# The second chunk's gate and up sums and masked product made in the opening stage, in two down banks, with first-pass weights in four slots

## The reference

```python
scores = softmax(x @ gate_w.T)                       # 64 experts in 8 groups of 8
w_e    = scores of the 8 largest, 0 elsewhere
flat   = w_e[:, inv_map];  scalar = flat.sum(-1)      # one number for each token and group
soft   = softmax(where(flat == 0, -1e9, flat), axis=-1)
xg = x[:, None, :] + einsum('ngi,ghi->ngh', soft, mask_up_w)
g  = einsum('ngh,gih->ngi', xg, gate_proj_w)          # 352 columns for each of 8 groups
u  = einsum('ngh,gih->ngi', xg, up_proj_w)
d  = einsum('ngi,ghi->ngh', silu(g) * u, down_proj_w)
y  = einsum('ng,ngh->nh', scalar, d)
```

## Time and profile before

| | us |
|---|---|
| median of 3 runs | 1887.09 |
| the profiled execution's own time | 1890.33 |
| its span, first to last instruction | 1888.6 |
| PE busy | 1857.5 |
| DVE busy | 801.9 |
| ACT busy | 527.9 |
| POOL busy | 128.2 |

### The profile page before, as it was taken

One profiled execution on the slowest core, in us unless ns is written; L12 is line 12 of the kernel. 1 busy time (PEld: TensorE's weight loads), 2 busy tenths in 40 slices (PEclk: granted clock), 3 DMA queues, 4 the chain that ended last, 5 costly groups with the idle time before them and its releaser, 6 DMA issues.

```text
span 1888.6 us, 22836 instructions
## 1 busy us (share of the span) xinstructions
PE 1857.5 (98%) x8896; PEld 1551.5 (82%) x8896; DVE 801.9 (42%) x1478; ACT 527.9 (28%) x801; POOL 128.2 (7%) x224
## 2 busy tenths in 40 slices
PE   5999999999999999999999999999999999999998
PEld 4888888888888888888888888888888888888887
DVE  5555554545354544323334455354544324322222
ACT  3334422533124432112212533123432111311111
POOL 1121110000000100000010000000000000000000
PEclk9999999999999999999999999999999999999999
DMA  5877786445664456576576555564455566567664
GB/s 169 309 266 262 277 292 207 153 149 176 209 222 157 151 168 205 182 257 210 209 246 220 168 191 167 187 231 167 157 171 178 203 237 212 207 227 254 224 235 160
DMA packets 93131, 390.68 MB, mean 207 GB/s; under 512 B 11584, under 2 KB 11968, under 8 KB 70496
## 3 DMA queue, kind: packets, MB, share of 16 engines
q1 hardware_dynamic: 54096, 286.74, 43.1%
q10 hardware_dynamic: 27600, 47.15, 9.1%
q0 software_dynamic: 11328, 55.32, 7.4%
HBM read 347.36 MB, written 41.81 MB: 206 GB/s over the span
## 4 chain that ended last, share of the span: by engine, by line
PE 95%; DVE 3%; ACT 1%; issue 1%; DMA 1%; SPq 0%; POOL 0%; DVEq 0%; ACTq 0%
PE bank L975 27%; PE bank L977 27%; PE bank L976 27%; PE bank L1203 4%; PE bank L985 1%; PE bank L1146 1%; PE bank L1145 1%; PE bank L1138 1%; PE bank L1132 1%; PE bank L1190 0%; DVE act_t L620 0%; PE bank L1191 0%; PE bank L1005 0%; PE bank L1022 0%; PE bank L1006 0%
## 5 line engine op out<-in xcount | busy, mean ns | idle before, releaser
L975 PE MATMUL bank<-x_hi,wt 128*128 128x512 f32 x1408 | 557.1, 396 | 2.7 <-ACT sig L554 2.7
L977 PE MATMUL bank<-x_lo,wt 128*128 128x512 f32 x1408 | 549.7, 390 | 0.0
L976 PE MATMUL bank<-x_hi,wt 128*128 128x512 f32 x1408 | 549.3, 390 | 0.0
L620 DVE TENSOR_TENSOR act_t<-bank,sig 128x512 f32<-128x512 f32 x176 | 121.6, 691 | 565.7 <-PE bank L1203 556.0
L977 PEld LDWEIGHTS bank<-x_lo,wt 128*128 128x128 f32 x1408 | 264.6, 188 | 56.9
L975 PEld LDWEIGHTS bank<-x_hi,wt 128*128 128x128 f32 x1408 | 265.0, 188 | 55.0 <-issue 2.9
L976 PEld LDWEIGHTS bank<-x_hi,wt 128*128 128x128 f32 x1408 | 265.1, 188 | 52.3
L975 PE MATMUL bank<-dt,a_hi 128*128 128x512 f32 x704 | 279.2, 397 | 0.3 <-DVE a_lo L620 0.3
L977 PE MATMUL bank<-dt,a_hi 128*128 128x512 f32 x704 | 275.1, 391 | 0.0
L976 PE MATMUL bank<-dt,a_lo 128*128 128x512 f32 x704 | 274.2, 389 | 0.0
L554 ACT ACTIVATE sig<-bank 128x512 f32<-128x512 f32 x176 | 105.4, 599 | 484.2 <-PE bank L1203 484.1
(11 more groups left out here) (168 smaller groups left out, 1709.6 us busy)
## 6 DMA issues: line engine op xcount, KB each, us to landing
wt<-scr_w SPq DMA_DIRECT2D x154, 1152.0 KB, 5.2
dt<-scr_d SPq DMA_DIRECT2D x154, 512.0 KB, 5.1
s_bc<-scr_s ACTq DMA_DIRECT2D x128, 256.0 KB, 5.3
scr_w<-wt POOLq DMA_DIRECT2D x22, 1152.0 KB, 6.5
state<-wat POOLq DMA_DIRECT2D x28, 512.0 KB, 5.4
b_all<-wgu SPq DMA_DIRECT2D x22, 512.0 KB, 5.5
scr_d<-dt POOLq DMA_DIRECT2D x22, 512.0 KB, 5.4
s_bc<-scr_s ACTq DMA_DIRECT2D x32, 192.0 KB, 4.7
```

The source lines that it names most:

```text
L620: return nc.vector.tensor_tensor(dst, a, b, op)
L975: mm(dst, wh, xh, start=start, stop=False)
L976: mm(dst, wl, xh, start=False, stop=False)
L977: return mm(dst, wh, xl, start=False, stop=stop)
```

## The change

Five edits, all in phase 0 but the third:

- `masked(1)` and both sums of chunk 1 move from the loop into the opening stage. The sums go to `YB[0]` and `YB[1]` (`g_bank`, `u_bank`), which are free until the first `down`; `down(0)` therefore moves behind both sums of chunk 2 and runs just ahead of `down(1)`.
- High and low gate/up weights of the first pass lie in four slots (`first_w`: two of `wt`, two of `tw`) where they had two; the mask parts stay in two. Chunk 2's weights are split in the opening stage (`gu_hi(2)`, `gu_lo(2)`). The store is now two DMAs, `store_w` (1 MB) and `store_m` (128 KB).
- Router step 46 makes the transposes, the copy and the store of the group sums, ahead of the group softmax rows (49, 50); step 51 is gone, and the sum itself (`scal`) moves from the end of step 46 to the end of step 44 on DVE. This holds for all phases.
- A one-column Silu (`warm`) right behind the Exp of the opening stage.
- The load of block 1 (1 MB, `x_t[1]`) moves from the opening stage to behind `raw(2)` on SP's queue; that of block 2 stays behind `raw(4)`.

```diff
+        def g_bank(n):
+            return YB[0] if n == 1 else GB
+        def u_bank(n):
+            return YB[1] if n == 1 else UB
+        def first_w(c):
+            return (wt, tw)[c % 4 // 2][:, c % 2, 0:2 * GW]
...
@@ SP @@
             raw(1)
-            sp.dma_start(xr(1), x_t[1]).then_inc(ld_x[1], 16)
             for c in range(2, CH):
                 raw(c)
+                if c == 2:
+                    sp.dma_start(xr(1), x_t[1]).then_inc(ld_x[1], 16)
                 if c == 4:
                     sp.dma_start(xr(2), x_t[2]).then_inc(ld_x[2], 16)
@@ POOL @@
             for c in range(CH):
-                store(c)
+                if c == 0:
+                    store_w(0)
+                if c + 1 < CH:
+                    store_w(c + 1)
+                store_m(c)
                 store_d(c)
@@ ACT @@
-            for k in range(43, SLOTS):
-                router(0, k)
+            router(0, 43)
+            gu_hi(2)
+            router(0, 45)
+            act.wait_ge(pool_init, 1)
+            nc.scalar.activation(warm[:], mhalf[:, 0:1], ACT.Silu)
+            router(0, 46)
+            m_top(1)
             load_s(0)
+            router(0, 49)
+            router(0, 50)
             load_s(1)
...
-                    if p == 0 and 0 < c < CH - 1:
+                    if p == 0 and 1 < c < CH - 1:
                         gu_hi(c + 1)
...
-                    if p == 0 and c + 1 < CH:
+                    if p == 0 and 0 < c < CH - 1:
                         m_top(c + 1)
@@ DVE @@
             m_mask(0)
-            router(0, 43)
-            router(0, 44)
             m_rest(0)
-            for k in range(45, SLOTS):
+            m_mask(1)
+            for k in range(43, SLOTS):
                 router(0, k)
+            m_rest(1)
+            gu_lo(2)
...
-                    if p == 0 and c + 1 < CH:
+                    if p == 0 and 0 < c < CH - 1:
                         m_mask(c + 1)
                         m_rest(c + 1)
@@ PE @@
+            router(0, 43)
+            masked(1)
             pe.wait_ge(perm_ok, 4)
-            for k in range(43, SLOTS):
-                router(0, k)
+            router(0, 44)
+            main(g_bank(1), 0, 0, 1)
+            router(0, 46)
+            main(u_bank(1), P, 0, 1)
+            router(0, 49)
+            router(0, 50)
...
-                    if n:
-                        pe.wait_ge(sig_ok, n)
+                    if n > 1:
+                        pe.wait_ge(sig_ok, n if n > 2 else 1)
                         main(GB, 0, p, c)
-                    soft(GB, 0, p, c).then_inc(g_ok, 1)
+                    soft(g_bank(n), 0, p, c).then_inc(g_ok, 1)
...
+                    if n == 2:
+                        pe.wait_ge(sig_ok, 2)
+                        pe.wait_ge(t1_ok, 2)
+                        down(0)
+                    if n > 1:
                         down(n - 1)
                     pieces(3 * n + 2)
-                    if p == 0 and c + 1 < CH:
+                    if p == 0 and 0 < c < CH - 1:
                         masked(c + 1)
```

More of the change, by code:

```diff
@@ L124, in build @@
         ms = sb("ms", [P, NT])
+        warm = sb("warm", [P, 1])
         rr = sb("rr", [P, NT])
@@ L161, in build @@
         d_in = [sem(f"d_in{i}") for i in range(2)]
-        st_w = [sem(f"st_w{i}") for i in range(2)]
+        st_w = [sem(f"st_w{i}") for i in range(4)]
+        st_m = [sem(f"st_m{i}") for i in range(2)]
         st_d = [sem(f"st_d{i}") for i in range(2)]
@@ L239, in load_w @@
                 n, half = p * CH + c, c % 2
+                if p == 1 and c < 4:
+                    sp.wait_ge(st_w[c], 16 * len(range(c, CH, 4)))
                 if p == 1 and c < 2:
-                    sp.wait_ge(st_w[half], 16 * HALF)
+                    sp.wait_ge(st_m[half], 16 * HALF)
                 sp.wait_ge(u_ok, n - 1)
@@ L290, in rstd_of, with store_w, store_m @@
                 pool.wait_ge(rstd_ok, (r + 1) * NT)
-            def store(c):
-                half = c % 2
+            def store_w(c):
                 pool.wait_ge(gu_lo_ok, c + 1)
+                pool.dma_start(scr_w[c][:, 0:W_M], first_w(c).bitcast(F32)).then_inc(st_w[c % 4], 16)
+            def store_m(c):
                 pool.wait_ge(m_ok, c + 1)
-                pool.dma_start(scr_w[c], wt[:, half, :].bitcast(F32)).then_inc(st_w[half], 16)
+                pool.dma_start(scr_w[c][:, W_M:WW], wt[:, c % 2, W_M:WW].bitcast(F32)).then_inc(st_m[c % 2], 16)
             def store_d(c):
@@ L397, in t_hi @@
                     act.wait_ge(v_mm, 2 * t + 2)
+                elif t == 0:
+                    act.wait_ge(u_ok, CH)
+                    act.wait_ge(st_w[2 + s], 16 * len(range(2 + s, CH, 4)))
                 elif s == S_V:
-                    wait(act, k_mm, t * H)
-                elif t:
+                    act.wait_ge(k_mm, t * H)
+                else:
                     act.wait_ge(wo_ok, t * NT)
@@ L553, in silu @@
                 wait(act, t1_ok, n)
-                nc.scalar.activation(sig[:], GB[:], ACT.Silu).then_inc(sig_ok, 1)
+                nc.scalar.activation(sig[:], g_bank(n)[:], ACT.Silu).then_inc(sig_ok, 1)
             def round_a(n):
@@ L1023, in router @@
                     ins.then_inc(flat_ok, 1)
-                elif k in (49, 50, 51):
+                elif k == 46:
+                    pe.wait_ge(scal_ok, p + 1)
+                    for j in range(NT):
+                        ins = nc.tensor.transpose(W1[0:G, cols(j)], scal[:, j, :], ident[:])
+                    ins.then_inc(scalT_ok, 1)
+                elif k in (49, 50):
                     i = k - 49
@@ L1194, in main @@
             def main(b, c0, p, c):
-                hi, lo, _ = weights(c)
+                hi, lo = weights(p, c)
                 for k in range(KC):
```

78 lines of the change are left out of this document (38 added, 40 removed).

## The result

The changed kernel takes 1883.97 us (median of 22 runs, 1881.85 to 1888.72) against 1887.14 (22 runs, 1886.38 to 1893.75). The medians differ by 3.2 us. The ratio is 0.9981, 0.19% less, with a 95% interval of 0.9975 to 0.9986, that is 2.6 to 4.7 us.

The account below looks back on a forecast made before the run. PE was taken to bound the kernel, busy 1857.5 of 1888.6 us. The walk's 6.2 us gain, cut to 5.65 at chunk 3 and 4.95 at chunk 5, gave 1887.09 - 4.9 = 1882.2, range 1880.0 to 1884.9.

Parts of the forecast that it names:

- The end of routing: Opening stage: step 44 at 27.1 us, PE filled with moved work, all four `soft` products done at 36.6.
- The group row: Group sums copied near 32.9 us, multiply of chunk 0 at 38.4, 3.9 earlier; no drain of 1.38 counted.
- The wait that takes their place: Ahead of chunk 2's `soft`: PE idle from 40.35 to 47.1 us for `m_rest(2)`, 6.7 against 11.7 before.
- The clock: Behind chunk 2's idle spell: low for 3.1 us as before; restored at once 1.6 shorter, low twice as long 1.6 longer.
- Chunk 3's load behind the block: Gate/up load on SP's queue: issued at 42.0 us, landing 12.7 later; `soft` of chunk 3 at 61.7, gain 5.65.
- From ACT's start to PE's `soft`: At chunk 3, from the landing of its weights to PE's `soft`: 7.0 us, from 6.95 in the earlier trace.
- The same again at chunk 5: Load behind the second block: issued at 61.3 us, landing at 74.7, `soft` at 81.7, gain down to 4.95.
- Edits at nothing: Split store, moved `scal`, step 46's copy in later phases: no cost; last two, uncovered, under 0.5 us at one chunk.
- Rival 1: Weights of chunks 3 and 5 late, landings of 12.7 to 13.4 us; gain 4.3 to 5.6, 1881.5 to 1882.8; chance 0.50.
- rival 3: Gain mostly given back by longer loads, low clock or late group row; gain 1 to 3.7 us; chance 0.16.
- Rivals 2, 4 and 5: No collision at the block, 1879.3 to 1880.9 (0.24); nothing gained (0.05); slower through chunk 3's load stalling ACT (0.05).

Follow-up runs that it names:

- m_first: The changed kernel with `m_rest(2)` made between the two multiplications of chunk 0, not behind chunk 1's splits; 1885.25 us, ratio 0.9985.
- The fill: x_open plus 24 products of no use on PE in the idle spell ahead of chunk 2's `soft`; 1880.38 us, ratio 0.9958.
- m_store_ahead: The changed kernel with each chunk's mask store queued ahead of the next chunk's 1 MB store; 1883.29 us, ratio 0.9975.
- after_again: The changed kernel timed again with no edit; 1883.95 us, ratio 0.9982.
- after_third: The changed kernel timed a third time with no edit; 1884.14 us, ratio 0.9983.
- x_open: The changed kernel with block 1's load back in the opening stage; 1883.34 us, ratio 0.998.
- m_first_x_open: The changed kernel with the edits of m_first and x_open together; 1876.63 us, ratio 0.9944.
- m_first_gu3: m_first with chunk 3's gate/up load issued ahead of `raw_d(2)` and the block, once `gu_lo(1)` is done; 1877.39 us, ratio 0.9938.
- sums_only: The kernel before plus only the earlier group sums (`scal` in step 44, new step 46, `load_s(0)` ahead of `softT`); 1882.2 us, ratio 0.9967.
- sums_only_2: sums_only timed again, beside after_third; 1882.55 us, ratio 0.9972.

## Why the prediction was right, and where its terms were off

1882.2 was forecast and 1883.97 measured, inside the range. The chance of 0.72 for faster by over 0.2% was too high: the ratio, 0.19% below one, falls just short of it, with the bound inside its interval. Step by step:

- **The end of routing**: right. Step 44 at 26.95 (27.1), four `soft` from 35.43 to 36.6 (36.6), the clock full to 40 us.
- **The group row**: right and 0.75 cautious. Copy at 32.09, multiply of chunk 0 at 37.65 (38.4), 0.5 of it since the spread landed 3.5 us after its issue (34.18 to 37.65), not 4.0, and 0.3 since it was issued sooner (34.18, not 34.5). The pause that the Trainium skill (ScalarE: Activation LUTs, What ACT_TABLE_LOAD costs) adds to a load isn't in this trace either: the load starts at 30.69, 0.02 after the Exp ends, and the Silu at 31.98, as the load of 1.28 ends.
- **The wait that takes their place**: right. `m_rest(2)` releases PE at 46.38 (47.1) after 6.09 idle (6.7). m_first shows by taking it away that this wait is real, and that another stands behind it.
- **The clock**: mis-sized, with little effect on the result. I took the 3.1 us at the low level over from before, with "low twice as long" as the other bound; it was 5.9 us, so that bound held. The fill shows a price of 2.6 us on PE's path, where I had counted 1.6. But in the change chunk 3's weights arrive behind PE's own path, so most of that price is hidden. In m_store_ahead the low level lasted 3.2 us (the window below), and PE only waited longer, 1.38 us, with `soft` of chunk 3 at 62.08:

```profile
46.61:49.79 3.18, 3.18 (x8) 2.50 (x9) 0.00 (x0) 0.60 (x1) 0.54 (x1) 0.50 0.99 381
```

- **Chunk 3's load behind the block**: right. Issued at 41.37 (42.0), landed after 13.0 (12.7); in after_again after 12.4, in after_third after 11.8. Taking the block away alone (x_open) gives 0 to 1.1, on top of m_first 8.5 at chunk 3. The fit of the Trainium skill (DMA: Bandwidth & Descriptors, Anatomy of one DMA — SWDGE (gpsimd) path) is for one DMA on GpSimd's queue; the estimate from it for these three loads, which go by SP's queue, is 6.2 us, and the measurement decides, with 13.0.
- **From ACT's start to PE's `soft`**: mis-sized. I counted 7.0; it took 8.4, the difference being the 1.47 that ACT stood behind the issue of two spreads (58.02). The chunk from which I read the 7.0 issues one spread there (0.34 us at 83.33 in before). `soft` of chunk 3: 61.7 forecast; 62.76, 62.60 and 61.55 in three traces. In the first, an issue 0.6 sooner, a landing 0.3 longer and these 1.4 make up the 1.1 of lateness: the gain there is 4.6, not 5.65.
- **The same again at chunk 5**: wrong in mechanism, small in size. The gate/up load behind block 2 was issued at 62.35 and was there when ACT came for it at 73.43, in at most 11.1 us, where I had taken 13.4. I had added a loss of 0.7 and the traces show 0.1. A wait at chunk 5 occurs only where PE is further ahead (m_first_x_open, m_first_gu3).
- **Edits at nothing**: neither was nothing. The split store costs 0.3 to 0.5 us at chunk 22 in the change, up to 1.6 in relatives of it, as m_store_ahead shows. I had named a slot's reuse four chunks later, not the mask store's place behind the next chunk's store on its own queue. And the lead grows behind chunk 22, where I expected no change: by 0.15 to 0.21 us in each of phases 1, 2, 4 and 5, 0.6 to 0.8 in all, in every trace of a kernel with the new step 46, sums_only included. That fits `scal` and step 46 in later phases, but only one trace of before stands against them, so it isn't shown. Another 0.3 comes at chunk 91 in the change, where the time between two `soft` moves by up to 1.2 us from one execution to another, with and without the change (9.59 us in the first trace of the change, 9.87 in before, 10.85 in sums_only_2).

So the 4.9 of the sum and the 4.9 at the last `soft` of the first trace agree in part by luck. The forecast had a lead of 5.65 at chunk 3, 4.95 at chunk 5 and the same to the end; the trace has 4.6, 4.5, then 4.0 at chunk 22 and back to 4.9 by a gain that the sum did not hold. What was right is the path: which wait takes the place of the old ones, and what comes late behind it.

The medians give 2.8 to 3.7 against three sets of runs of before. The two profiled executions lie 7.0 apart in their own times (1890.33 and 1883.30), 3.9 more than the medians: that of before took 3.2 more than its median, that of the change 0.7 less. Of the 7.0, 4.9 are the lead and 2.1 the end of the kernel behind the last issue (below). That leaves a lead of 4.9 against 3.2 in the medians, a little outside the interval of 2.6 to 4.7, and why stays open.

Rival 1 is the mechanism at chunk 3, but the measured 1883.97 lies outside its 1881.5 to 1882.8 and inside the 1883.4 to 1886 of rival 3, whose clock "low twice as long" came true as well. Rivals 2, 4 and 5 did not.

## What to carry to other kernels

Before moving work into an idle spell, follow the order on to the next two points where the engine waits: here PE's idle before the routing transposes was filled and a new spell opened ahead of chunk 2, and the short edit that brought the latest arrival forward (the group sums) was worth as much alone. Waits in series must be relieved together, and an edit that shows nothing alone (m_first) may be most of the gain with its partner. Where a load or store is put on a queue, look at what small transfer stands behind it, what the queue waits for before it, and who waits for the small one.

## What the runs showed of the hardware

- The kernel ends at one of two distances behind the issue of the same last store. In before, SP's last issue ends at 1884.26 and the span at 1888.6, 4.3 us later; in the change 1879.33 and 1881.6, 2.3 us. Over all fourteen traces it is 2.2 to 2.3 us in nine and 4.1 to 4.4 in five, and after_again and after_third (4.4) are the same kernel as the change. A single pair of spans can be off by 2 us for that alone.
- How long the lower clock level outlasts an idle spell doesn't follow from the length of that spell. It held for 5.9 us of work after 6.1 us idle in the change, 3.2 after 5.9 in m_store_ahead, and 3.1 after 2.15 in before. These are the windows shown; in the change and in before the low level goes on for 0.2 and 0.4 us more.
- A 512 KB load issued behind 256 KB and the 1 MB block of tokens was there after 11.8 to 13.0 us (the change's three traces, DMA share 0.96 in the window of 46.4 to 52.3). With the block gone it took 5.3 (41.32 to 46.59 in m_first_x_open).
- The issue of two small spreads on ACT's queue took 1.66 us at 58.02, where single ones took 0.33 to 0.35, and ACT's next instruction waited 1.47 for it. In x_open the same pair took 0.81 us (55.47) and the wait was 0.65; why is open.
- The opening moves between executions: step 44 came at 26.95 in the change and at 27.66 in sums_only, though `masked(1)` stands ahead of it in the change alone.
